# A gated cross-attention block in fp32 on one Trainium2 core: feed-forward rows transposed by VectorE in 32 x 32 squares and placed through memory, instead of by TensorE

## The reference, cut to what matters

```python
x = x + tanh(g_xattn[0]) * attention(layernorm(x), ctx, wq, wk, wv, wo)   # k = [ctx, xn @ wk.T], v = [ctx, xn @ wv.T]
h = relu((layernorm(x) @ sign(up_weight).T) * up_scale)                   # hidden 2048
x = x + tanh(g_ffn[0]) * (h @ sign(down_weight).T) * down_scale * output_scale
```

## Time and profile before

| | |
|---|---|
| median of 3 runs | 595.32 us (595.18 to 595.76) |
| the profiled execution | 595.3 us, its span 593.5 us |
| PE busy | 586.2 us, 99% of the span |
| DVE, ACT, POOL busy | 377.8, 290.3, 116.8 us |
| HBM | 36.45 MB read, 6.30 MB written |

### The profile page before, as it was taken

How to read it: one execution, slowest core, us unless ns; L and a number is a source line. 1 busy time by engine, 2 the same in 40 slices (tenths; PEclk the granted TensorE clock), 3 DMA queues, 4 the chain that set the end, 5 groups by cost and what they waited for, 6 DMA issues and landing times.

```text
span 593.5 us, 7100 instructions
## 1 busy us (share of the span) xinstructions
PE 586.2 (99%) x2738; PEld 486.2 (82%) x2738; DVE 377.8 (64%) x532; ACT 290.3 (49%) x426; POOL 116.8 (20%) x111
## 2 busy tenths in 40 slices
PE   8999999999999999999999999999999999999997
PEld 7888888888888888888888888888887888888885
DVE  5889454687443677544677786755459734766654
ACT  3875421555231655230556565655559445645531
POOL 5006403011003021003020025242322003242001
PEclk9999999999999999999999999999999999999999
DMA  7714121212020242020222222120211302231011
GB/s 287 244 55 142 39 73 67 71 37 71 2 72 0 63 159 99 1 71 2 71 72 71 83 75 91 35 72 35 72 36 35 141 1 72 76 138 36 0 72 71
DMA packets 20097, 43.21 MB, mean 73 GB/s; under 512 B 4832, under 2 KB 4832, under 8 KB 19680
## 3 DMA queue, kind: packets, MB, share of 16 engines
q1 hardware_dynamic: 20064, 42.76, 21.4%
HBM read 36.45 MB, written 6.30 MB: 72 GB/s over the span
## 4 chain that ended last, share of the span: by engine, by line
PE 97%; DVE 2%; DMA 0%; ACT 0%; issue 0%
PE proj L540 35%; PE score L670 19%; PE turn L655 12%; PE score L573 9%; PE score L540 7%; PE proj L655 5%; PE proj L573 4%; PE turn L532 3%; PE score L804 2%; PE proj L638 1%; PE turn L638 1%; DVE rows L1660 1%; DMA rows<-in_x 0%; DVE scaled L1657 0%; DVE stats L1483 0%; PE score L811 0%
## 5 line engine op out<-in xcount | busy, mean ns | idle before, releaser
L670 PE MATMUL score<-down_signs,hid_split 128*128 128x512 f32 x512 | 133.7, 390 | 0.8 <-DVE scaled L1541 0.7
L670 PEld LDWEIGHTS score<-down_signs,hid_split 128*128 128x128 f32 x512 | 95.9, 188 | 21.6 <-DVE scaled L1541 1.1
L540 PE MATMUL proj<-probsT,four_x 128*128 128x512 f32 x384 | 89.3, 391 | 0.0
L540 PEld LDWEIGHTS proj<-probsT,four_x 128*128 128x128 f32 x384 | 71.5, 188 | 14.6
L540 PE MATMUL proj<-four_x,weights 128*128 128x512 f32 x336 | 76.8, 389 | 0.0
L540 PEld LDWEIGHTS proj<-four_x,weights 128*128 128x128 f32 x336 | 63.0, 188 | 13.0
L465 POOL TENSOR_TENSOR four_x<-raw_ctx,four_x 128x2048 fp32r<-128x2048 f32 x7 | 32.6, 4657 | 189.5 <-ACT four_x L892 189.5
L1536 DVE TENSOR_TENSOR hid_split<-hid,hid_split 128x512 fp32r<-128x512 f32 x64 | 44.4, 695 | 17.1 <-ACT hid_split L1115 17.0
L540 PE MATMUL proj<-weights,four_x 128*128 128x512 f32 x192 | 51.9, 405 | 0.0
L655 PE MATMUL turn<-ops_b,up_ops 128*128 128x512 f32 x192 | 51.7, 391 | 0.0
L900 ACT ACTIVATE four_x<-proj 128x512 fp32r<-128x512 f32 x32 | 19.1, 597 | 65.8 <-PE proj L540 65.8
(11 more groups left out here) (128 smaller groups left out, 865.3 us busy)
## 6 DMA issues: line engine op xcount, KB each, us to landing
raw_w<-in_ffn_w SPq DMA_DIRECT2D x24, 512.0 KB, 3.3
raw_ctx<-in_ctx_turned SPq DMA_DIRECT2D x4, 1024.0 KB, 5.5
raw_ctx<-in_ctx SPq DMA_DIRECT2D x4, 1024.0 KB, 5.7
result<-rows SPq DMA_DIRECT2D x16, 256.0 KB, 2.0
rows<-in_x SPq DMA_DIRECT2D x3, 1024.0 KB, 6.1
turned_x<-in_x_turned SPq DMA_DIRECT2D x3, 1024.0 KB, 5.3
rows_away<-rows SPq DMA_DIRECT2D x1, 2048.0 KB, 12.0
rows<-rows_away SPq DMA_DIRECT2D x1, 2048.0 KB, 7.9
```

The lines of the kernel that those rows point to most:

```text
L540: last = pe.matmul(bank, lhs(l), rhs(r), start=start and i == 0, stop=stop and i == 2)
L670: last = pe.matmul(wide(r), hid_split[:, n % HR, s, r * P:(r + 1) * P], down_signs[:, chunk_of(q), :], start=(q == 0 and s == HI), stop=(q ...
```

## The change

- **Turning.** PE no longer turns any feed-forward row: `turn_block_rows`, its PSUM banks, waits and ACT copies go. DVE normalizes a tile and transposes it in 32 x 32 squares (`turn_squares`: a `tensor_scalar` and a `transpose` of 128 x 512). SP stores the squares of a batch in four DMAs (`store_squares`: 1 MB in all, in runs of 128 bytes) to a DRAM array in which each square stands at its transposed place, and loads the batch back, 1 MB, to `raw_x` (`block_rows_back`).
- **When.** Batches 0 and 1 are turned in attention batches 1 and 2 (`turn_pair_squares`) and come back in the last batch, when the probabilities are turned. Batch 2 is turned after groups 1 and 2, batch 3 after groups 3 and 4; before its first tile DVE waits until batch 2's store has landed, since both use one buffer.
- **Signs.** Four down blocks (2, 6, 3, 7) are taken at the ends of groups 0 to 3, each just ahead of that group's up block.
- **Probabilities.** Their 8 transposing jobs run as two runs of four, after the second and the fourth value product, in four banks; the new side's jobs come first.
- **Pair's end.** The last 8 down products run in the order PAIR_END, and DVE scales the first finished tiles ahead of the LO parts.

```diff
+        squares_v = block_rows.rearrange("b (j a) (r i n) -> b i a r j n", a=SQ, i=P // SQ, n=SQ)
+        PAIR_END = [(HC - 2, 0), (HC - 2, 1), (HC - 1, 0), (HC - 1, 1), (HC - 2, 2), (HC - 1, 2), (HC - 2, 3), (HC - 1, 3)]
-        SIGNS = [("down", i) for i in range(HG - 1)] + [("up", 0), ("down", HG - 1)] + [
-            ("up", g) for g in range(1, 2 * HG)]
+        SIGNS = [("down", 0), ("down", 4), ("down", 1), ("down", 5), ("up", 0), ("up", 1)]
+        LATE_DOWN = (2, 6, 3, 7)
+        for i, block_index in enumerate(LATE_DOWN):
+            SIGNS += [("down", block_index), ("up", i + 2)]
+        SIGNS += [("up", g) for g in range(2 + len(LATE_DOWN), 2 * HG)]
-        TURN_ORDER = ((2, NEW), (2, OLD), (3, NEW), (3, OLD), (0, NEW), (1, NEW), (0, OLD), (1, OLD))
+        TURN_ORDER = ((2, NEW), (3, NEW), (0, NEW), (1, NEW), (2, OLD), (3, OLD), (0, OLD), (1, OLD))
...
+            def store_squares(b, squares):
+                sp.wait_ge(block_turned, RT * (b + 1))
+                for i in range(P // SQ):
+                    sp.dma_start(squares_v[b, i], squares[i * SQ:(i + 1) * SQ].rearrange(
+                        "a r (j n) -> a r j n", n=SQ)).then_inc(squares_out[b], 16)
+            def block_rows_back(b):
+                sp.wait_ge(squares_out[b], STORED)
+                sp.dma_start(raw_x[b // 2][:, b % 2], block_rows_v[b]).then_inc(block_in[b], 16)
...
-            for n in range(HG + 11):
-                load_signs(n)
+            for n in range(4):
+                load_signs(n)
+            sp.wait_ge(turned, TURNS_ALL)
+            block_rows_back(0)
+            block_rows_back(1)
+            for n in range(4, signs_at("up", 4)):
+                load_signs(n)
+            store_squares(2, late_squares)
+            load_signs(signs_at("down", 7) - 1)
+            load_signs(signs_at("up", 5) - 1)
+            sp.wait_ge(rows_spilled, 16)
+            block_rows_back(2)
+            load_signs(signs_at("up", 6) - 1)
+            load_signs(signs_at("up", 7) - 1)
+            store_squares(3, late_squares)
+            block_rows_back(3)
...
                     for i, (lhs, rhs) in enumerate(v_terms(r)):
                         last = product(proj_bank(proj0(b) + r), lhs, rhs, i == 0, i == DC - 1)
-                        if i == 1:
-                            turn_probs(b, 2 * r)
                     last.then_inc(proj_done, 1)
-                    turn_probs(b, 2 * r + 1)
+                    if r == 1:
+                        pe.wait_ge(score_sums, 10 * (b + 1))
+                        for i in range(RT):
+                            turn_probs(b, i)
+                    if r == 3:
+                        for i in range(RT, 2 * RT):
+                            turn_probs(b, i)
...
+                if g < len(LATE_DOWN):
+                    take_signs(signs_at("down", LATE_DOWN[g]) - 1)
                 act.wait_ge(up_sums, sum_done(g, AT_C12))
                 relu(hid1(2 * j), hid1(2 * j), j)
...
+            def turn_squares(f, tile_normed, squares):
+                dve.wait_ge(block_rstd_done, f // RT + 1)
+                dve.tensor_scalar(tile_normed, rows[:, f, :], block_mean_var[:, f % RT, 0:1],
+                                  block_rstd[:, f % RT:f % RT + 1], ALU.subtract, ALU.mult).then_inc(block_normed, 1)
+                dve.wait_ge(block_normed, f + 1)
+                dve.transpose(squares, tile_normed).then_inc(block_turned, 1)
+            def turn_late_squares(f):
+                if f == 3 * RT:
+                    dve.wait_ge(squares_out[2], STORED)
+                for i in (f, f + 1):
+                    turn_squares(i, late_normed[:, i % 2, :], late_squares[:, i % RT, :])
...
             for q in range(HC):
+                if q < 2:
+                    scale_even(0, 2 * q)
                 hidden_low(1, q)
-                if q == 0:
-                    scale_even(0, 0)
-                if q == 1:
-                    scale_even(0, 2)
```

More of the change, by code:

```diff
@@ L405, in _ @@
                     sp.dma_start(raw_ctx[:, :, :], ctx_turned_v[b + 1]).then_inc(ctx_in, 16)
+                if b in (1, 2):
+                    store_squares(b - 1, pair_squares)
             sp.wait_ge(scored, product_scored(BATCH - 1, S3, 1))
-            for n in range(HG + 11):
+            for n in range(4):
[14 more added lines that the diff above has]
+            block_rows_back(3)
+            for n in range(signs_at("up", 8) - 1, HG + 11):
                 load_signs(n)
@@ L715, in up_group @@
                 piece(2)
-                if pair == 0 and j in TURNED_IN:
-                    pe.wait_ge(raw_out, TURNED_IN[j] + 1)
-                    turn_block_rows(TURNED_IN[j] + 1, proj[:, (g + 1) % 2, :])
                 pe.wait_ge(p1_out, g + 1)
@@ L861, in _ @@
                 up_group(0, j, down_of_two(0, j - 1))
-            for i in range(2 * RT):
-                down_of_two(0, HG - 1)(i)
+            for q, r in PAIR_END:
+                down(0, q, r)
             for q in range(HC - 2):
@@ L869, in _ @@
                 up_group(1, j, down_of_two(2, j - 1))
-            for i in range(2 * RT):
-                down_of_two(2, HG - 1)(i)
+            for q, r in PAIR_END:
+                down(2, q, r)
             for q in range(HC - 4):
@@ L990, in take_signs @@
                 act.activation(dst, raw_w[:, :], ACT.Sign).then_inc(signs_ready, 1)
-            def block_rows_out(f, bank):
-                act.wait_ge(turned, TURNS_ALL + f + 1)
-                act.activation(raw_x[f // (2 * RT)][:, f // RT % 2, :, f % RT * P:(f % RT + 1) * P], four(bank), ACT.Copy
-                               ).then_inc(raw_out, 1)
-            def two_rows_out(f):
-                for i in (f, f + 1):
-                    block_rows_out(i, turn[:, i % 2, :])
             def right_high(pair, i):
                 if i in (B11, B21):
-                    act.wait_ge(raw_out, 2 * RT * pair + RT)
+                    act.wait_ge(block_in[2 * pair], 16)
                 elif i == B22:
-                    act.wait_ge(raw_out, 2 * RT * pair + 2 * RT)
+                    act.wait_ge(block_in[2 * pair + 1], 16)
                 else:
@@ L1036, in batch @@
                 proj_out(m + 1, new_side[:, HI, 1, :])
-                probs_out(b, 3)
-                probs_out(b, 4)
+                for i in range(RT):
+                    probs_out(b, i)
                 proj_out(m + 2, new_side[:, HI, 2, :])
@@ L1464, in batch @@
                             next_rows_low(b + 1)
+                        if e == 2 and b >= 1:
+                            turn_pair_squares(b - 1)
                 if last_batch:
```

194 lines of the change are left out of this document (88 added, 106 removed).

## The result

The changed kernel takes **598.12 us** (median of nine runs, 595.36 to 599.21) against 595.24 us (nine runs, 595.04 to 595.88): ratio 1.0035, 95% interval 1.0021 to 1.0049. It is 0.35% slower. The forecast was 592.4 us, faster; its range held the time. The runs of before spread over 0.8 us, those of the change over 3.9 us, and that spread turns out to be part of the answer.

The account below looks back on a forecast made before the run. The prediction took PE, busy 99% at full clock, to bound the kernel; -7.4 - 0.5 - 1.3 + 5.9 + 0.4 = -2.9 us gave 592.4 us, 0.5% faster, with a range of 588.0 to 602.8.

Parts of the forecast that it names:

- 16 jobs of transposes: Last batch's attention product and groups 1, 2, 5, 6: removing PE's row transposes gains 7.4 us.
- Probabilities: Attention: transposing the probabilities in two runs of sixteen gains 0.5 us (0 to 0.7).
- the cover of 0.1 to 0.6 us: Attention: PE's 4.5 us of other work outlasts DVE's emptying of the second four banks by 0.1 to 0.6 us.
- The pair's end: First pair's end: reordered down products and earlier DVE scalings remove PE's wait, -1.3 us (0 to -1.3).
- Squares in attention: Attention batches 1 and 2: DVE's statistics, normalizations and transposes fit its idle time; cost 0, transpose taken as 0.6 us.
- Batch 2's store: From group 3: stores ahead in the queue delay down block 7's load, adding 0.4 us in group 4.
- The very slow and slow stores: Stores of 128-byte pieces: over 740 us if very slow (chance 0.05), 602.8 us if slow (chance 0.23).
- Two takes from one buffer: Ends of groups 0 to 3: up load waits for the down take, delaying PE's P2, +5.9 us in all.
- +1.76 us for the groups that follow groups 1, 2 and 3: P2 of groups 2 to 4: p1_copy comes late, so PE starts P2 at 410.83 instead of 409.07.
- The rivals on stores: Batch stores' 128-byte pieces move slower than forecast: 602.8 us (chance 0.23) or over 740 us (chance 0.05).
- the slow store's own sum: At 13 us of store data: load 7.9 late, second store 2.9 more, total +7.5, 602.8 us; chance 0.23.
- second take hidden: Group ends: faster sign load or earlier ACT hides the up block's take, 586.1 to 587.6 us; chance 0.13.

Follow-up runs that it names:

- experiment 1: The change with its four late down-block takes moved to mid-group, batch 2's squares one group earlier and its stores spread around a load: 586.37 us, ratio 0.9848.
- experiment 2: The change plus 2, 8, 12 and 8 matmuls with unread results ahead of P2 in groups 1 to 4: 594.26 us, ratio 0.9981.
- experiment 7: The change with early down-block takes except group 2's, squares and stores moved, so PE meets one gap: 591.25 us, ratio 0.994.
- experiment 6: The change with all four takes still late, but batch 2's squares made earlier and its stores spread around a load: 596.29 us, ratio 1.0013.
- experiment 8: The change with squares and stores moved, only group 2's take late, and 7 matmuls with unread results put in that gap: 589.37 us, ratio 0.9895.
- Experiment 4: The kernel before with only the signs' order changed to four late down-block takes; PE still transposes rows, no stores of squares: 603.44 us, ratio 1.0140.
- experiment 9: The change with early down-block takes except group 0's, squares and stores moved, leaving one short gap: 586.9 us, ratio 0.9858.

## Why the prediction was wrong

It said faster where the change is slower, and its number was 5.7 us too low. By its own steps:

- **16 jobs of transposes, -7.4**: right. -3.6 by group 1, -1.9 in groups 1 and 2, -1.9 in groups 5 to 7, and experiment 1, with all three gains and no waits, comes out at -9.0 for -9.2.
- **Probabilities, -0.5**: right within what can be read (4.14 gained for 3.63 + 0.5). No wait showed in attention; the cover of 0.1 to 0.6 us held.
- **The pair's end, -1.3**: right, -1.26 measured alone.
- **Squares in attention, 0**: right. The transpose that no row had shown takes 0.71 us where 0.6 was taken. The last one ends at 176.69 and the LO part that it precedes starts at 176.72, where it started at 176.86 before, so the squares fit the idle time with nothing to spare:

```profile
175.98 0.71 DVE L1394 STREAM_TRANSPOSE pair_squares<-pair_normed 128x512 f32<-128x512 f32 x1
```

- **Batch 2's store, +0.4, as a late load of down block 7**: this place was wrong. That take was on time. What came late was the up load just ahead of it, which ran beside the store (4.29 us for 3.36), so the third wait is 2.75 us instead of 1.76. That the store did it is likely, not shown. The very slow and slow stores did not come.
- **Two takes from one buffer, +5.9 (0.6 and three times 1.76)**: the waits are 0.54, 1.78, 2.75 and 1.78, 6.9 in all; less the 1.0 of the slower load that is 5.9. The working was right to 0.1 us, its price was not. **The step that failed is "+1.76 us for the groups that follow groups 1, 2 and 3": it sold idle time of TensorE at its length.** Everything up to there summed over a PE at full clock, which the page of before showed in all 40 slices, and that was true of a PE that in the feed-forward waited once, for 0.71 us. After three of the four gaps that the change makes, the granted clock fell for some microseconds. This cost 5.1 us in the profiled run, 3.9 by the medians of the change and its filled form (experiment 2), and 1.7 after the one gap of experiment 7. The sum had no term for it.

With what was measured, the sum closes on the profiled execution: 593.5 - 9.2, plus 6.9 of waits, 5.1 of lower clock and the 0.9 of other slow matmuls, is 597.2 us, for a span of 597.4. Runs of this one program spread over 3.9 us.

- **The rivals on stores**: 256 KB in pieces of 128 bytes landed in 4.7 us, beside 4.3 for 512 KB of signs. The factor of 19 that the Trainium skill ("DMA: Bandwidth & Descriptors", Rules for kernel authors) gives is for transposing by a plain DMA with a rearranged access pattern instead of by the hardware's DMA transpose. Here VectorE had transposed within the squares and the DMA only placed runs of 128 bytes, and no run sets that factor against this store. In the slow store's own sum, 13 + 12.4 + 1.6 - 24.0 is 3.0 us and not 2.9, which changes nothing. The rival that came nearest is "second take hidden", 586.1 to 587.6 us: not in the change, but experiment 1 makes it so by hand, at 586.4.

What stays open: what sets whether a gap is followed by the lower clock, and for how long. Gaps of 1.64 and 1.83 us passed without one in experiment 6, one of 1.79 in 8; gaps of 1.82 and 1.78 did not pass in 7 and in the change, and executions of one program differ. Experiment 4's profiled run let four pass, of 0.64 to 1.81 us. Also open is why an identical load took 3.36 us in experiment 7 and 4.92 in experiment 8, and 4.29 in the change for some 3.2 in its filled form.

## What to carry to other kernels

Where one engine is at full clock because it is never idle, a wait that a change adds is not worth its length: against experiment 1, one gap of 1.8 us cost 3.5 us (experiment 7, profiled run), gaps of 6.0 us in all cost 8.5 (experiment 6, profiled run) and of 6.9 cost 12.8 (the change, profiled run), while one of 0.5 us cost just its length (experiment 9). When two loads share one buffer, place each take where its engine idles anyway: with takes of 1 us moved a few microseconds ahead, and stores moved that alone gave 1.8 us (experiment 6), a loss of 0.35% became a gain of 1.5%. A kernel whose runs spread widely beside a neighbour whose runs don't may have a clock that moves.

## What the runs showed of the hardware that was not expected

- The granted clock fell to its lower level after gaps of 1.8 to 2.8 us, one alone included: matmuls of 128 x 512 went from 0.227 to some 0.41 us. It fell not in the gap but within 1.7 us after PE had resumed (in the change, 385.75 to 387.42 behind the second gap), and each fall in the change cost 1.7 us of full-speed work. Whether it falls varies from run to run of one program (593.7 to 598.6 us in experiment 6).
- Behind a wait the first four matmuls take 1.20 us instead of 0.91 even at clock 1.00, and also where the wait had been filled with other matmuls (experiment 2).
- Work whose result is thrown away made the kernel faster: 30 matmuls, 6.8 us of busy time, for -3.9 us.
- SyncE needs time to issue a store of 2048 pieces: in the change four such took 5.2 us of its own time, about 1.3 us each, against 0.33 us for one load of signs behind an idle queue (experiment 7).
- The load of 512 KB of signs, with stores of small pieces issued behind it, took some 3.2 us (experiment 2), 3.36 (7), 4.29 (the change) and 4.92 (8).
- A 32 x 32 transpose pass of VectorE over 128 x 512 of four bytes takes 0.71 us in the change, like a two-input pass (0.69).
